# A hybrid block on one core: the rope partner copied across partitions by ScalarE, and the linear attention's stacks two heads deep with products in two row halves

## What is computed

```
x = x + attn_a(layernorm(x))      # linear attention, 16 heads of 16, with 4 memories
x = x + ffn(layernorm(x))         # ternary weights, 1024 hidden
x = x + attn_b(layernorm(x))      # softmax attention, rope, causal
x = x + ffn(layernorm(x))

# attn_a, per head (elu1 = elu + 1):  sq = elu1(q); sk = elu1(k)
num = einsum('bhsd,bhsde->bhse', sq, cumsum(sk x v));  den = sq . cumsum(sk)
# rope in attn_b, on q and k, pairs of neighbouring features:
y_even = cos * x_even - sin * x_odd
y_odd  = sin * x_even + cos * x_odd
```

## Time and profile before

| | before |
|---|---|
| time, median of 3 runs | 2647.59 us (2646.87 to 2655.3) |
| the profiled execution: its time, its span | 2646.55 us, 2644.8 us |
| PE busy over the span | 2151.8 us, 81% |
| DVE busy | 1723.8 us, 65% |
| ACT busy | 1308.6 us, 49% |
| POOL busy | 970.2 us, 37% |
| mean granted PE clock | 0.926 |

### The profile page before, as it was taken

One profiled execution on the slowest core, in us unless ns is written; L12 is line 12 of the kernel. 1 busy time (PEld: TensorE's weight loads), 2 busy tenths in 40 slices (PEclk: granted clock), 3 DMA queues, 4 the chain that ended last, 5 costly groups with the idle time before them and its releaser, 6 DMA issues.

```text
span 2644.8 us, 54601 instructions
## 1 busy us (share of the span) xinstructions
PE 2151.8 (81%) x18402; PEld 1414.8 (53%) x18402; DVE 1723.8 (65%) x4346; ACT 1308.6 (49%) x2630; POOL 970.2 (37%) x852
## 2 busy tenths in 40 slices
PE   0567979888897988889898988989798888988676
PEld 0435555655565565555555555555555555655333
DVE  6637766667676667767666776667676676766241
ACT  1333645646464554646455464636546364644423
POOL 2434252533425253342525344242534324252201
PEclk9878999989898999989999999989999999999878
DMA  2313233333232333323133333313333332223030
GB/s 91 49 28 58 52 49 57 49 65 57 42 53 46 57 52 70 50 54 53 34 57 58 65 49 65 53 34 52 59 57 49 66 57 42 52 46 49 17 49 9
DMA packets 121770, 135.68 MB, mean 51 GB/s; under 512 B 16912, under 2 KB 102544, under 8 KB 121488
## 3 DMA queue, kind: packets, MB, share of 16 engines
q1 hardware_dynamic: 110736, 115.08, 27.8%
q10 hardware_dynamic: 10752, 16.78, 1.7%
HBM read 80.95 MB, written 41.94 MB: 46 GB/s over the span
## 4 chain that ended last, share of the span: by engine, by line
issue 48%; POOL 18%; PE 17%; DVE 8%; ACT 5%; DMA 2%; SPq 1%; POOLq 0%; ACTq 0%; DVEq 0%
PE bank L1252 6%; POOL place L603 5%; POOL place L593 5%; POOL place L614 3%; POOL rstd L578 2%; POOL bsl L618 2%; PE bank L1397 2%; PE bank L1206 2%; ACT place L670 2%; POOL place L639 1%; ACT place L700 1%; ACT place L703 1%; PE bank L1265 1%; PE bank L1310 1%; DVE stats L898 1%
## 5 line engine op out<-in xcount | busy, mean ns | idle before, releaser
L1139 DVE TENSOR_REDUCE mxs<-bank 128x1 f32<-128x128 f32 (+3 forms) x1024 | 428.5, 482 | 199.5 <-PE bank L1399 199.2
L803 ACT ACTIVATE place<-bank 128x512 f32<-128x512 f32 (+1 forms) x768 | 352.0, 548 | 254.4 <-PE bank L1413 253.4
L603 POOL TENSOR_TENSOR place<-am,place 128x512 f16<-128x512 f32 x256 | 290.5, 1156 | 274.1 <-ACT place L715 266.1
L578 POOL TENSOR_TENSOR rstd<-ve,halfc 128x4 f32<-128x4 f32 x64 | 64.9, 1015 | 615.7 <-DVE ve L905 615.7
L715 ACT ACTIVATE place<-am 128x512 f16<-128x512 f32 x256 | 149.5, 624 | 283.6 <-DVE am L964 283.6
L1411 PE MATMUL bank<-qst,kst 128*128 128x512 f16 (+3 forms) x1024 | 239.3, 304 | 41.6 <-DMA qst<-nmt 25.8
L1265 PE MATMUL bank<-w2q,place 128*128 128x256 f16 x2048 | 253.0, 276 | 20.6 <-POOL place L593 17.4
L1397 PE MATMUL bank<-kst,qst 96*128 96x128 f16 (+3 forms) x1024 | 240.7, 306 | 23.8 <-DMA kst<-scratch 10.8
L964 DVE SCALAR_TENSOR_TENSOR am<-bank,tri 128x512 f32<-128x512 f32 x256 | 167.1, 685 | 102.4 <-PE bank L1282 63.2
L1265 PEld LDWEIGHTS bank<-w2q,place 128*128 128x128 f16 x2048 | 197.3, 99 | 61.5 <-issue 26.1
L1206 PE MATMUL bank<-ident,place 128*128 128x128 f32 x512 | 101.1, 336 | 149.8 <-ACT place L670 146.3
(11 more groups left out here) (159 smaller groups left out, 4634.9 us busy)
## 6 DMA issues: line engine op xcount, KB each, us to landing
scratch<-place SPq DMA_DIRECT2D x128, 256.0 KB, 2.3
qst<-scratch SPq DMA_DIRECT2D x256, 128.0 KB, 5.4
kst<-scratch SPq DMA_DIRECT2D x256, 128.0 KB, 6.0
xa<-x SPq DMA_DIRECT2D x16, 512.0 KB, 3.6
xc<-xb ACTq DMA_DIRECT2D x16, 512.0 KB, 2.9
out<-xc ACTq DMA_DIRECT2D x16, 512.0 KB, 4.4
qst<-wall SPq DMA_DIRECT2D x8, 256.0 KB, 8.2
qst<-nmt SPq DMA_DIRECT2D x128, 4.0 KB, 1.7
```

Of the source, the lines that this page charges most:

```text
L603: G.tensor_tensor(alp[:, n % 2, k, :], am[:, k, :], ahp[:, n % 2, k, :], ALU.subtract).then_inc(s["al"], 1)
L803: A.activation(pf[h % SLOTS][:, S2_COL[k]:S2_COL[k] + S2_W[k]], bank_of(L2, ("S2", h, k))[:, 0:S2_W[k]], ACT.Exp, scale=D ** -0.5 / RS ** ...
L1139: V.tensor_reduce(mxs[:, g:g + 1], bank_of(L2, ("S1", n, k))[:, Q_AT[i]:Q_AT[i] + (i + 1) * P], AX, ALU.max).then_inc(s["mx"], 1)
```

## The change

Two parts, and with them the table of due times and the constant `CUT` (5 before, 7 after).

**Rope.** The swapped weights `BQR`, `BKR` are gone; there is one projection per half. The weight columns of BQ and BK are sorted at setup so that even features come out on partitions 0 to 63 and odd ones on 64 to 127 (`split_by_parity`), and the cos and sin tables are loaded in the same order. ACT copies each half of the PSUM bank into the other half's partitions of an SBUF buffer (two instructions of 64 partitions by 512), POOL multiplies that by sin and then adds DVE's cos product. The buffer is now double. Since a head's features now stand in two places, each of lane 2's stack DMAs is two of 8 partitions each.

**Stacks of lane 1.** Two heads stand above each other, on partitions 0 to 63 and 64 to 127, so there are no zero rows, no memsets of them at setup, and half as many columns. `products` contracts over 64 partitions, alternating between the upper and the lower half; the two halves go to different banks. Lane 1's stack DMAs are also two for one, of four head pairs each. The causal blocks are found by `h % 2` and `h // 2` in place of `h // 4` and `h % 4`.

```diff
-AQ, AK, AV, AO, BQ, BK, BV, BO, BQR, BKR = range(10)
-NMAT = 10
+AQ, AK, AV, AO, BQ, BK, BV, BO = range(8)
+NMAT = 8
+PAIR = P // 2
-LANDED = 2 * 4 * 16
+LANDED = 2 * 4 * 2 * 16
-CUT = 5
+CUT = 7
-            "N": [110.9, 112.9, 125, 130.9, 138.7, 0, 4.4, 10.7, 13.8, 19.7],
+            "N": [101.4, 103.5, 112.6, 119, 123.4, 128.8, 132.8, 0, 4.8, 9.3],
...
-    jobs += [(("PB", t, r), "t12", 2 * t + r + 1) for t in range(4) for r in range(2)]
+    jobs += [(("PB", t), "t1", t + 1) for t in range(4)]
...
# SP, stack
-                        sp.dma_start(dst[to, heads, :], L.scratch[half, part, :, which, :]
-                                     .rearrange("(h d) s -> d h s", d=D)).then_inc(L.landed[half], 16)
+                        rows = L.scratch[half, part, :, which, :]
+                        for r in range(2):
+                            if L is L1:
+                                to = slice(r * PARTS + k * D, r * PARTS + (k + 1) * D)
+                                sp.dma_start(dst[to, pairs, :], rows.rearrange("(g r d) s -> r d g s", r=2, d=D)[r]
+                                             ).then_inc(L.landed[half], 16)
+                                continue
+                            to = slice(k * D + r * D // 2, k * D + (r + 1) * D // 2)
+                            sp.dma_start(dst[to, heads, :], rows.rearrange("(r h i) s -> r i h s", r=2, h=HH8)[r]
+                                         ).then_inc(L.landed[half], 16)
# POOL, setup
-            for st in (L1.qst, L1.kst):
-                G.memset(st[PARTS:P, :, :].rearrange("p a s -> p (a s)").bitcast(F32), 0.0).then_inc(pool_const, 1)
# POOL, lane 2
-                    pool.wait_ge(s["t12"], due(L2, "t12", t, 2 * q + 2))
-                    G.tensor_tensor(L2.sq[:, q, :], t12[:, 0, :], t12[:, 1, :], ALU.add).then_inc(s["y"], 1)
+                    pool.wait_ge(s["xs"], due(L2, "xs", t, 2 * q + 2))
+                    G.tensor_tensor(t12[:, q % 2, 1, :], t12[:, q % 2, 1, :], sint[:, :], ALU.mult).then_inc(s["t2"], 1)
+                    pool.wait_ge(s["t1"], due(L2, "t1", t, q + 1))
+                    pool.wait_ge(s["t2"], due(L2, "t2", t, q + 1))
+                    G.tensor_tensor(L2.sq[:, q, :], t12[:, q % 2, 0, :], t12[:, q % 2, 1, :],
+                                    ALU.add).then_inc(s["y"], 1)
# ACT, lane 2
+                        act.wait_ge(s["pr"], due(L2, "pr", t, q + 1))
+                        if q >= 2:
+                            act.wait_ge(s["y"], due(L2, "y", t, q - 1))
+                        for r in range(2):
+                            to, of = slice(r * PAIR, (r + 1) * PAIR), slice((1 - r) * PAIR, (2 - r) * PAIR)
+                            A.activation(t12[to, q % 2, 1, :], bank_of(L2, ("PB", q))[of, :], ACT.Copy,
+                                         scale=RS / WS).then_inc(s["xs"], 1)
# DVE, lane 2
-                    for r in range(2):
-                        dve.wait_ge(s["pr"], due(L2, "pr", t, 2 * q + r + 1))
-                        if q >= 1 and r == 0:
-                            dve.wait_ge(s["y"], due(L2, "y", t, q))
-                        V.scalar_tensor_tensor(t12[:, r, :], bank_of(L2, ("PB", q, r))[:, :], RS / WS,
-                                               (cost, sint)[r][:, :], ALU.mult, ALU.mult).then_inc(s["t12"], 1)
+                    dve.wait_ge(s["xs"], due(L2, "xs", t, 2 * q + 2))
+                    V.scalar_tensor_tensor(t12[:, q % 2, 0, :], bank_of(L2, ("PB", q))[:, :], RS / WS, cost[:, :],
+                                           ALU.mult, ALU.mult).then_inc(s["t1"], 1)
# PE, lane 1
-                for k in range(2):
-                    into = take(L1, ("PR", n, k), t)
-                    for h4 in range(4):
-                        h = half * HH8 + 4 * k + h4
-                        ins = T.matmul(into[:, h4 * P:(h4 + 1) * P], L1.kst[0:STK, h, cols], L1.qst[0:STK, h, cols],
+                into = [take(L1, ("PR", n, r), t) for r in range(2)]
+                for g in range(NT):
+                    pair = half * HH8 // 2 + g
+                    for r in range(2):
+                        rows = slice(r * PARTS, (r + 1) * PARTS)
+                        ins = T.matmul(into[r][:, g * P:(g + 1) * P], L1.kst[rows, pair, cols], L1.qst[rows, pair, cols],
                                        start=True, stop=True)
# PE, lane 2
-                    project(L2, ("PB", q, 0), a, m, "pr", t)
-                    project(L2, ("PB", q, 1), b, m, "pr", t)
+                    project(L2, ("PB", q), mat, m, "pr", t)
```

More of the change, by code:

```diff
@@ L36 @@
 PARTS = 4 * D
+NP = NH // 2
 STK = 96
@@ L110 @@
[L110 to L115, removed]
[5 rows of a table added]
+            "FTR": [23.7],
+            "FTT": [26.9],
+            "DN": [48.1, 50.7],
+            "T": [58.5],
+            "TR": [63.3],
+            "TT": [71.5],
+            "PA": [80.6, 82.5, 84.8, 86.4, 88.1],
+            "V": [92.8, 94.6],
+            "RM": [97.2],
@@ L353, in build @@
             L.xlo = own("xlo", [P, KH, S], F16)
-            L.qst = own("qst", [P, NH, S], F16)
-            L.kst = own("kst", [P, NH, S], F16)
+            stacks = NP if L is L1 else NH
+            L.qst = own("qst", [P, stacks, S], F16)
+            L.kst = own("kst", [P, stacks, S], F16)
             L.oth, L.otl = L.xh, L.xlo
@@ L444, in sequence @@
             return of[bass.ds(t, 1)].rearrange("o p j f -> p (o j) f")
[L447 to L448 removed]
+        w_stage = [t[:, :, :].rearrange("p a b -> p (a b)").bitcast(F32) for t in (L1.qst, L1.kst)]
         f_stage = L2.qst[:, :, :].rearrange("p a b -> p (a b)").bitcast(F32)
@@ L469, in _ @@
             sp.dma_start(b2bc[:, :], b2.broadcast_to([P, H])).then_inc(c_in, 16)
-            sp.dma_start(cost[:, :], cos).then_inc(c_in, 16)
-            sp.dma_start(sint[:, :], sin).then_inc(c_in, 16)
+            for table, of in ((cost, cos), (sint, sin)):
+                for r in range(2):
+                    sp.dma_start(table[r * PAIR:(r + 1) * PAIR, :],
+                                 of.rearrange("(n r) s -> r n s", r=2)[r]).then_inc(c_in, 16)
             sp.wait_ge(pool_const, 1)
@@ L775, in lane2 @@
                 turned(L2, 0, t)
-                for q in range(4):
-                    yield at2("PB", q)
-                    act.wait_ge(s["y"], due(L2, "y", t, q + 1))
-                    A.activation(L2.sth[:, q, :], L2.sq[:, q, :], ACT.Copy).then_inc(s["sh"], 1)
+                for q in range(5):
+                    if q < 4:
+                        yield at2("PB", q)
+                        act.wait_ge(s["pr"], due(L2, "pr", t, q + 1))
[5 more added lines that the diff above has]
+                                         scale=RS / WS).then_inc(s["xs"], 1)
+                    if q >= 1:
+                        yield at2("PH", q - 1)
+                        act.wait_ge(s["y"], due(L2, "y", t, q))
+                        A.activation(L2.sth[:, q - 1, :], L2.sq[:, q - 1, :], ACT.Copy).then_inc(s["sh"], 1)
                 for j in range(2):
@@ L1302, in outputs @@
                     for part in (ahp, alp):
-                        ins = T.matmul(local[:, h * VW:(h + 1) * VW], part[:, n % 2, h // 4, (h % 4) * P:(h % 4 + 1) * P],
+                        ins = T.matmul(local[:, h * VW:(h + 1) * VW], part[:, n % 2, h % 2, (h // 2) * P:(h // 2 + 1) * P],
                                        L1.vp[:, c, half * HH8 + h, :],
```

207 lines of the change are left out of this document (107 added, 100 removed), and 18 rows, old and new, of the table MARKS.

## The result

| | before | after |
|---|---|---|
| time, median of 4 runs each | 2650.3 us (2646.9 to 2655.3) | 2711.5 us (2696.9 to 2713.5) |
| ratio | | 1.0218, 95% interval 1.0177 to 1.0258 |
| the profiled execution: time, span | 2646.55, 2644.8 | 2710.77, 2708.7 |
| head, to the first start of lane 2 | 234.5 | 238.0 (forecast 236.9) |
| mean of 14 periods | 152.2 | 156.4 (forecast 145.5) |

A forecast was written before the change was run, and what follows sets the result against it. PE, busy 132.8 of 151.9 us per period, was taken as the bound. Head 236.9, loop 2037.3 (14 periods each 6.7 shorter), sequence 14 139.3 and last 135.9 gave span 2549.4, time 2552 us; forecast 2530 to 2580, chance 0.62.

The forecast's parts named there:

- The stack DMAs: Stack loads of both lanes: transfer, not issue, sets the time; 0.5 us lost per period, bounds none to 3.7 later.
- The sign that I had named for it: PE's wait for kst<-scratch above 3 us per period would show that the slower DMA rival holds.
- The slower rival: Half-size stack DMAs take as long as full ones, PE stalls 11 us per period: 2706 us, chance 0.06.
- PE's work: PE per period: 5.3 us less from rope projections and 1.0 from products, together 6.3 us less.
- PE's idle share: Loop period: PE's idle share stays, so the period falls by 7.2 us, 6.7 after 0.5 for the landing.
- the rival in which latency eats it: Longer rope step and new order leave PE waiting; period falls 2 to 4 us: 2604 us, chance 0.20.
- Products: Lane 1's products in row halves on PE: 1.0 us gained per period, bounds 2.4 gained to 0.5 lost.
- The stage costs nothing: Rope step, 1.8 us longer through ACT and POOL: costed at nothing; 0.5 to 2 us per period if cover goes.
- Setup and head: Before the loop: setup 3 us shorter, CUT adds 4.4, landings 1; head from 234.5 to 236.9 us.
- ACT, POOL and DVE: Busy time per period: ACT near 86 us, POOL near 65, DVE near 103, all far below PE.

The follow-up runs named there:

- 5: Kernel before, old order, with only lane 1's stacks two deep, their DMAs two of 16 partitions, and products in row halves: 2641.2 us, ratio 0.9988.
- 4: Two runs of DMA shapes alone, computing nothing of the reference, 2 MB of 1 KB rows per phase: 16 partitions by 8 rows 112 GB/s, 8 by 8 65.
- 1: Changed kernel with features sorted by parity, pair, head, so lane 2's stack DMAs are whole again, of 16 partitions: 2598.9 us, ratio 0.9821.
- 2: Kernel before with each of lane 2's stack DMAs made two of 8 partitions, nothing else changed: 2788.0 us, ratio 1.0519.
- 3: Repaired kernel with each of lane 2's stack DMAs made two of 16 partitions by 4 heads: 2579.7 us, ratio 0.9743.
- repaired kernel: The kernel of 1: changed kernel with lane 2's stack DMAs whole again through another feature order, 2598.9 us.
- 9: Repaired kernel with each rope projection computed twice into its bank, giving PE its 24 matmuls per sequence back: 2637.0 us, ratio 0.9958.
- 7: Order and parts separated, lane 2's DMAs whole, against kernel before: new order alone 2631.3 us; rope alone 2685.6 in old order, 2599.3 in new; both in old 2681.3.
- 6: Repaired kernel with the four products of the upper partition half first, then the four of the lower: 2603.3 us, ratio 0.9825.
- 8: Rope part alone in the old order (2685.6 us): smaller lane 2 stack DMAs 2681.6 us; instead two due times moved ahead of lane 1's norm, 2632.9 us, ratio 0.9939.

## Why the prediction failed, step by step

**The stack DMAs: the step that failed.** I wrote that "the transfer, 1 MB in 11 us, sets the time, not the issue", gave it 0.5 us per period, and took the same rate for any DMA of the same bytes. For lane 1 that was right: sixteen DMAs of 16 partitions cost nothing (5). For lane 2, whose new DMAs have 8, the rate fell to 65 to 68 GB/s from 108 to 112, at a share of 0.54 instead of 0.96 (4), and the term is 156.4 - 149.1 = 7.3 us per period, 113 us in all (1; 2 shows it without the rest of the change). The sign that I had named for it came, a wait for kst<-scratch above 3 us per period: 7.1. I had both shapes in the diff and put them together as "half-size".

**The slower rival** had the place, PE standing still at lane 2's first scores, and with 2706 nearly the time. It had the wrong property: halved DMAs are harmless, halved partitions are not (3, 4). That its time came so near is luck: it starts from 2552, 47 us below the repaired kernel's 2599, and its stall of 11 us per period is 3.7 above the 7.3 measured; the two errors nearly cancel.

**PE's work** fell nearly as worked out: 125.6 us per period in the repaired kernel against 132.8 - 6.3 = 126.5. The step from there to the period was mis-sized. I kept PE's idle share, 7.2 us; with whole DMAs the period fell by 3.1. The 24 matmuls are worth 2.4 us per sequence, not 5.3 (9), for they stood under a chain of copies, products, bounce and landing that ends only 2.3 us sooner without them. That is the rival in which latency eats it: 2604, measured 2599. The idle time is at the chain's end: in the repaired kernel PE is busy 58% of the time from 16 to 32 us after a sequence's start, 83% before (mean of five sequences).

**Products.** 1.0 us was taken; PE's busy time fell by 0.3 to 0.7, depending on the stretch, the time by nothing clear (5, 7). In PE's timeline of the changed kernel a group of eight at full clock now stands so:

```profile
1144.70 0.59 PE L1285 MATMUL bank<-xlo,w1q 128*128 128x512 f16 x2
1145.22 0.40 PE L1316 MATMUL bank<-qst,kst 64*128 64x128 f16 x8
1145.56 0.40 PE L1332 MATMUL bank<-place 128*128 128x264 f16 x2
```

0.34 us to the next start instead of 0.46, and 0.52 from the two 512-column matmuls ahead, which cost 0.44: some 0.08 us is lost on the way in, not the 0.2 taken from the earlier trace rows, and 0.12 is won. But my reason for the gain is not borne out. With the four products of one half ahead of the four of the other (6) a group takes 0.35:

```profile
1131.65 0.41 PE L1319 MATMUL bank<-qst,kst 64*128 64x128 f16 x8 [1.66 <-issue]
1132.00 0.40 PE L1335 MATMUL bank<-place 128*128 128x264 f16 x2
```

So the alternating of neighbours wins at most 0.01 us per group; what wins the rest stays open.

**"The stage costs nothing"** held only by the order. I named a price of 0.5 to 2 us if the cover went, and looked on ACT and POOL at what queues behind the new instructions. What cost 3 us per period in the old order was the reverse: the new instructions behind a waiting norm (8).

**The rest.** Setup and head 238.0 (forecast 236.9), ACT, POOL and DVE within 1 us. The order by itself is worth 15 us (7), for which my sum had no term of its own.

## What to carry to other kernels

Read a DMA's shape, not only its bytes: cutting one along the partitions from 16 to 8 halved the busy share of the DMA engines and cost 7 us per sequence, while cutting it along the rows cost nothing. Work taken from the busiest engine is worth only what it shortens the chain beside it: here 2.4 us of 5.3. When a step moves to other in-order engines, look for waiting instructions ahead of it in their streams; two due times decided between 1.4% slower and 0.6% faster.

## What was unexpected in the hardware

- The same DMAs of 8 partitions by 8 rows moved 65 GB/s issued by SP, and 110 issued by SP and ACT in turn, at the same share of the DMA engines (0.54 and 0.49). With 16 partitions it was 112 and 137.
- 32 partitions by 4 or 8 rows moved 193 and 184 GB/s, where 16 by 8 moved 108 to 112 at about the same share: the single engine was faster.
- An issue on SP took 0.35 us for 8 partitions by 8 rows and 0.47 for 16 by 4 in the changed kernel. Alone (4) it was 0.52 and 0.47.
- The same matmuls kept PE busy for 2.9 us per period more in the changed kernel than in the repaired one, with the granted clock at 0.90 instead of 0.92: the stall went together with a lower clock and longer work.
